# Last rounded layer of a 12-stage kernel: two of VectorE's steps move to GpSimd, one chunk ahead

## The reference, cut to what matters

```python
def _mx_quantize(t, eps=1e-30):                    # blocks of 32
    scales = maximum(max(abs(blocks), axis=-1) / 7.5, eps)
    q = nearest_on_grid(blocks / scales[..., None], GRID)   # 6-bit floats
    return q, scales
xq, xs = _mx_quantize(x2)
wq, ws = _mx_quantize(w2)
out = (xq * xs) @ (wq * ws).T + bias
...
x = x + 0.5 * _L3_ffn_ref(_layernorm(x), L3_ffn_weight, L3_ffn_bias)   # last line
```

## Time and profile before

| | |
|---|---|
| median of 3 runs | 2941.31 us |
| runs | 2941.31, 2930.59, 2941.32 us |
| the profiled execution's own time | 2940.02 us |
| its span in the profile | 2938.6 us |
| mean granted TensorE clock | 0.918 |

### The profile page before, as it was taken

How to read it: one execution, slowest core, us unless ns; L and a number is a source line. 1 busy time by engine, 2 the same in 40 slices (tenths; PEclk the granted TensorE clock), 3 DMA queues, 4 the chain that set the end, 5 groups by cost and what they waited for, 6 DMA issues and landing times.

```text
span 2938.6 us, 67913 instructions
## 1 busy us (share of the span) xinstructions
PE 2501.2 (85%) x25429; PEld 1983.4 (67%) x25429; DVE 2091.1 (71%) x7719; ACT 1766.2 (60%) x3449; POOL 1215.2 (41%) x1663
## 2 busy tenths in 40 slices
PE   7799998778699769459689999999999998895885
PEld 4467775455477547336479999999998896563664
DVE  6667765982377844664478888888988888446876
ACT  5444444533356334236369999999999995563553
POOL 4200002570274557575554442433244433556413
PEclk9789998978899879679889999999999998997997
DMA  9910000014310024225300000000010100441001
GB/s 237 277 44 3 3 3 1 6 46 128 110 34 14 31 76 137 80 88 160 109 19 16 19 21 14 21 14 14 14 35 23 36 23 12 131 147 31 25 6 30
DMA packets 126504, 164.60 MB, mean 56 GB/s; under 512 B 15457, under 2 KB 94946, under 8 KB 126178
## 3 DMA queue, kind: packets, MB, share of 16 engines
q1 hardware_dynamic: 98242, 86.58, 10.5%
q0 software_dynamic: 27936, 73.66, 8.3%
HBM read 85.18 MB, written 75.01 MB: 55 GB/s over the span
## 4 chain that ended last, share of the span: by engine, by line
PE 39%; DVE 13%; POOL 3%; issue 3%; ACT 1%; DMA 1%; DVEq 0%; POOLq 0%; ACTq 0%
PE banks L3643 7%; PE banks L3628 6%; PE banks L3573 3%; PE banks L3590 2%; PE banks L3609 2%; PE banks L3582 2%; PE banks L3566 2%; PE banks L3315 1%; PE banks L3317 1%; PE banks L3304 1%; PE banks L3305 1%; PE banks L3306 1%; PE banks L3608 1%; POOL bins L3269 1%; PE banks L3599 1%
## 5 line engine op out<-in xcount | busy, mean ns | idle before, releaser
L3643 PE MATMUL banks<-layer,shared_floats 128*128 128x128 f32 x2048 | 292.0, 275 | 0.0
L3643 PEld LDWEIGHTS banks<-layer,shared_floats 128*128 128x128 f32 x2048 | 258.8, 192 | 0.0
L3628 PE MATMUL banks<-shared_floats,layer 128*128 128x256 f32 x1024 | 243.9, 381 | 0.0
L4047 ACT ACTIVATE shared_floats<-banks,layer 128x256 f32<-128x256 f32 x512 | 210.1, 471 | 51.8 <-PE banks L3628 51.8
L3744 POOL TENSOR_SCALAR shared_floats<-shared_floats 128x2 f32<-128x2 f32 x256 | 58.2, 227 | 425.2 <-DVE shared_floats L3735 416.9
L3628 PEld LDWEIGHTS banks<-shared_floats,layer 128*128 128x128 f32 x1024 | 185.9, 192 | 20.2
L3746 POOL TENSOR_TENSOR shared_floats<-shared_floats,neg_half 128x2 f32<-128x2 f32 x256 | 184.1, 719 | 21.3
L3756 DVE TENSOR_SCALAR shared_floats<-banks,shared_floats 128x128 f32<-128x128 f32 x512 | 185.6, 404 | 6.9 <-POOL shared_floats L3746 6.9
L2213 DVE TENSOR_REDUCE shared_floats<-banks 128x2 f32<-128x512 f32 (+3 forms) x256 | 110.7, 485 | 93.1 <-PE banks L2077 91.7
L2318 ACT ACTIVATE shared_floats<-banks 128x480 f32<-128x480 f32 (+1 forms) x192 | 83.6, 488 | 143.9 <-PE banks L2084 143.9
L256 PE MATMUL banks<-ident,xn 128*128 128x128 f32 x320 | 61.1, 322 | 126.1 <-issue 76.3
(11 more groups left out here) (447 smaller groups left out, 7966.5 us busy)
## 6 DMA issues: line engine op xcount, KB each, us to landing
bins<-zero SPq DMA_DIRECT2D x1, 18176.0 KB, 69.7
layer<-in_dram_layers SPq DMA_DIRECT2D x16, 902.0 KB, 4.6
bins<-layer SPq DMA_DIRECT2D x16, 650.0 KB, 12.5
shared_floats<-bins SPq DMA_DIRECT2D x32, 325.0 KB, 3.9
expert_weights<-in_dram_experts SPq DMA_DIRECT2D x32, 312.0 KB, 3.1
outs<-shared_floats SPq DMA_DIRECT2D x16, 320.0 KB, 3.3
results<-zero SPq DMA_DIRECT2D x1, 4096.0 KB, 16.1
bins<-xn,f_bin_row POOLq DMA_INDIRECT x256, 2.3
```

What stands on the lines that cost most here:

```text
L3628: m = T.matmul(k.bank[5 + half][:, part], w["w1"][:, tile(n)], h1[:, :], start=True, stop=True)
L3643: m = T.matmul(to, hidden[:, n * S + t * P:n * S + (t + 1) * P], w["w2"][:, tile(n)], start=False, stop=(n == NF - 1), skip_group_check=True)
L4047: m = A.activation(hidden[:, n * S:(n + 1) * S], k.bank[5 + half][:, part], ACT.Gelu, bias=w["c1"][:, n:n + 1])
```

## The change

In the last stage alone, VectorE's rounding is split in three. `largest(i)` makes the scales and inverses, `widen(i)` the exponent bits, the magic number and its addition, and VectorE issues `largest(i + 1)` ahead of `widen(i)`. GpSimd makes the product with the inverse (`scale_blocks`, one chunk ahead) and the subtraction of the magic number (`subtract_magic`), before its multiplication by the scale. A second buffer each for the inverse and the magic number comes from arrays of the stage before, and ScalarE gets a wait for the product before it writes over a normalised buffer. `mix3` keeps `ffn3_quantise` as it was.

```diff
--- before.py
+++ after.py
@@ -828,6 +828,27 @@
     v.count(V.tensor_tensor(blocks(dst), blocks(src), spread(inverse), ALU.mult))
 
 
+def largest_of(k, src, scale, inverse, width):
+
+    V, v, nb = k.nc.vector, k.v, width // BLOCK
+    blocks = lambda ap: ap.rearrange("p (b k) -> p b k", k=BLOCK)
+    v.count(V.tensor_reduce(scale, blocks(src), AX.X, ALU.max, apply_absolute_value=True))
+    V.wait_ge(v.sem, v.n)
+    v.count(V.tensor_scalar(scale, scale, 1.0 / FP6_MAX, 1e-30, ALU.mult, ALU.max))
+    V.wait_ge(v.sem, v.n)
+    return V.reciprocal(inverse, scale)
+
+
+def add_magic(k, dst, magic):
+
+    V, v = k.nc.vector, k.v
+    v.count(V.tensor_scalar(magic.bitcast(U32), dst.bitcast(U32), 0x7F800000, None, ALU.bitwise_and))
+    V.wait_ge(v.sem, v.n)
+    v.count(V.tensor_scalar(magic, magic, 1.0, 1.5 * 2.0 ** 20, ALU.max, ALU.mult))
+    V.wait_ge(v.sem, v.n)
+    return V.tensor_tensor(dst, dst, magic, ALU.add)
+
+
 def to_six_bits(k, dst, magic):
 
 
@@ -878,6 +899,16 @@
     to_six_bits(k, xq[:, :], magic[:, :]).then_inc(k.sem("f3_rounded"), 1)
 
 
+def ffn3_inverse(k, n):
+
+    return (k.sb("f3_inverse", [P, CH // BLOCK]), k.sb("b3_tops", [P, 4 * BLOCKS]))[n % 2][:, 0:CH // BLOCK]
+
+
+def ffn3_magic(k, n):
+
+    return k.sb(("f3_magic", "b3_swapped")[n % 2], [P, CH])[:, :]
+
+
 def ffn3_multiply(k, engine, n):
 
     xq, scale = k.sb(f"f3_xq{n % 2}", [P, CH]), k.sb(f"f3_scale{n % 2}", [P, CH // BLOCK])
@@ -939,8 +970,24 @@
         V.scalar_tensor_tensor(out=k.chunk(i), in0=k.bank[4 + (s.c0 + i) % 2][:, :], scalar=0.5, in1=k.chunk(i),
                                op0=ALU.mult, op1=ALU.add).then_inc(k.sem("x_done"), 1)
 
+    def largest(i):
+        n = s.c0 + i
+        xn, inverse = k.sb(f"f3_xn{n % 2}", [P, CH]), ffn3_inverse(k, n)
+        V.wait_ge(k.sem("ln_xn"), s.ln(i) + 1)
+        if i >= 2:
+            V.wait_ge(k.sem("f3_scaled"), n - 1)
+        largest_of(k, xn[:, :], k.sb(f"f3_scale{n % 2}", [P, CH // BLOCK])[:, :], inverse, CH).then_inc(k.sem("l1_inverse"), 1)
+
+    def widen(i):
+        n = s.c0 + i
+        V.wait_ge(k.sem("l1_wide"), NC + i + 1)
+        add_magic(k, k.sb(f"f3_xq{n % 2}", [P, CH])[:, :], ffn3_magic(k, n)).then_inc(k.sem("f3_rounded"), 1)
+
+    largest(0)
     for i in range(NC):
-        ffn3_quantise(k, s, i)
+        if i + 1 < NC:
+            largest(i + 1)
+        widen(i)
         if i + 2 < NC:
             ln_stats(k, s, i + 2)
         if i:
@@ -953,6 +1000,8 @@
     k.nc.scalar.wait_ge(k.sem("x_done"), s.x0)
     ffn3_apply(k, s, 0)
     for i in range(NC):
+        if i + 1 >= 2 and i + 1 < NC:
+            k.nc.scalar.wait_ge(k.sem("l1_wide"), NC + i)
         if i + 1 < NC:
             ffn3_apply(k, s, i + 1)
         ffn3_copy(k, s.c0 + i, k.bank[2 + (s.c0 + i) % 2][:, :])
@@ -960,8 +1009,29 @@
 
 def ffn3_gpsimd(k, s):
 
+    G = k.nc.gpsimd
+
+    def scale_blocks(i):
+        n = s.c0 + i
+        xn, xq = k.sb(f"f3_xn{n % 2}", [P, CH]), k.sb(f"f3_xq{n % 2}", [P, CH])
+        G.wait_ge(k.sem("l1_inverse"), NC + i + 1)
+        G.wait_ge(k.sem("f3_turned"), n - 1)
+        G.tensor_tensor(tiles(xq[:, :], BLOCK), tiles(xn[:, :], BLOCK),
+                        ffn3_inverse(k, n).unsqueeze(2).broadcast_to([P, CH // BLOCK, BLOCK]), ALU.mult).then_inc(k.sem("l1_wide"), 1)
+
+    def subtract_magic(i):
+        n = s.c0 + i
+        xq = k.sb(f"f3_xq{n % 2}", [P, CH])
+        G.wait_ge(k.sem("f3_rounded"), n + 1)
+        k.g.count(G.tensor_tensor(xq[:, :], xq[:, :], ffn3_magic(k, n), ALU.subtract))
+        G.wait_ge(k.g.sem, k.g.n)
+
+    scale_blocks(0)
     for i in range(NC):
-        ffn3_multiply(k, k.nc.gpsimd, s.c0 + i)
+        if i + 1 < NC:
+            scale_blocks(i + 1)
+        subtract_magic(i)
+        ffn3_multiply(k, G, s.c0 + i)
         if i + 2 < NC:
             ln_shift(k, s, i + 2)
```

## The result

The changed kernel takes 2963.75 us, median of 5 runs (2956.59 to 2970.60); the kernel before, 2941.32 us in 5 runs beside it. The ratio is 1.0085, 95% interval 1.0067 to 1.0104: slower by 0.85%, as forecast (2965.9 us). The two medians lie 22.4 us apart, against 24.6 forecast. The profiled execution took 2967.28 us, its span 2965.8.

The account below looks back on a forecast made before the run. VectorE bounds the last stage at 5.96 us per chunk; the change closes a cross-engine ring of 9.09 plus 0.73 stall, 9.82 us, six times. With first and last turns it costs 24.6: 2941.3 becomes 2965.9 us, range 2952 to 2973.

Parts of the forecast that it names:

- to GpSimd, subtraction, to L916: Last stage: hand-over 0.09, GpSimd's subtraction 1.25, then 0.08 to its multiplication by the scale; 1.42 us.
- L916 to L191: Last stage, GpSimd: from the start of the multiplication by the scale to the start of the shift; 1.20 us.
- L191 to the end of L197: Last stage, GpSimd: the shift from first to last step, with VectorE idle beside it; 1.95 us.
- hand-over, norm, hand-over: Last stage: 0.09 to ScalarE, its four norms 1.65, 0.08 to VectorE; 1.82 us.
- The ring: Last stage: rounding chunk i queues behind a norm that follows from rounding chunk i - 1; 9.09 us, 9.82 with stall.
- The last turn: Last stage's final turn has no norm to wait for; chunk 7's multiplication ends 6.01 us after chunk 6's addition.
- The sum: Whole kernel: the change costs 24.6 us, so the median goes from 2941.3 to 2965.9 us, slower by 0.84%.
- The subtraction: GpSimd's subtraction of the magic number in the last stage, taken as 1.25 us between bounds 1.05 and 1.46.
- The stall: VectorE's rounding, starting second, waits for GpSimd's product to end; 0.73 us per turn, bounds 0 and 1.05.
- The rival in which GpSimd becomes the bound: Last stage: ring does not bind, GpSimd's own work sets 6.2 us a turn, 2945 us in all; chance 0.08.
- ScalarE's copy: Last stage: ScalarE's copy of chunk i lies beside GpSimd's shift and costs the ring nothing.
- The signs named for the profile: Last stage: VectorE's turn about 9.8 us, idle 4 to 5 us until the norm, subtraction near 1.25, L197 at 0.24.

Follow-up runs that it names:

- e3: Kernel before, nothing moved to GpSimd: VectorE makes scale, inverse and product of chunk i + 1 ahead of rounding chunk i; 2957.13 us, ratio 1.0058.
- e4: Changed kernel with GpSimd's product cut to the first 32 of 512 elements; 2955.36 us in one run.
- e7: Changed kernel with statistics and shift one chunk earlier, and ScalarE normalising chunk i + 2 ahead of its copy of chunk i; 2940.76 us, ratio 1.0004.
- e1: Changed kernel with statistics and shift made one chunk earlier; 2960.17 us, ratio 1.0066.
- e10: Changed kernel with only ScalarE's order changed, norm of chunk i + 2 ahead of the copy of chunk i; 2963.82 us in one run.
- e2: Changed kernel with VectorE rounding chunk i ahead of the block maximum of chunk i + 1, GpSimd's order kept; 2962.0 us in one run.
- e5: Kernel before in its old order, with only the subtraction of the magic number on GpSimd; 2929.21 us in one run.

## Why the prediction was right

The predicted median was 2965.9 us, the measured 2963.75. That the medians agree to 2 us is in part luck, since the start of the stage moves by more than that from profile to profile; what bears the prediction out are the steps inside the stage. By its own steps, in the changed kernel's turn from one addition (ends 2903.40) to the next (2913.09):

| step | predicted | measured |
|---|---|---|
| to GpSimd, subtraction, to L916 | 1.42 | 1.42 |
| L916 to L191 | 1.20 | 1.14 |
| L191 to the end of L197 | 1.95 | 1.96 |
| hand-over, norm, hand-over | 1.82 | 1.80 |
| block maximum, scale, inverse | 1.17 | 1.19 |
| exponent bits to the addition, with the stall | 2.26 | 2.18 |
| turn | 9.82 | 9.69 |

- **The ring**: right, and e3 shows it with nothing moved. The number of times it closes, six, is right too: chunk 0's addition ends 4.92 us after the stage's start (forecast 5.02), chunk 6's at 2951.81, so six turns take 58.1 us (58.9).
- **The last turn**: 6.01 us from chunk 6's addition to the end of chunk 7's multiplication, as forecast, with L845 at 1.11 and L847 at 1.15 us, both behind a GpSimd instruction. Behind it 7.98 us are left against 8.12 before.
- **The sum**: 24.6 forecast, 23.5 measured. The 1.1 us are 0.10 (first addition) + 0.83 (six turns) + 0.14 (what is left behind the last multiplication) from these lines.
- **The subtraction**: taken as 1.25 between bounds of 1.05 and 1.46; measured 1.26 to 1.27. The middle of two bounds was a choice, so that it fits to 0.02 is luck.
- **The stall**: forecast 0.73, and e4 takes 0.73 off the turn. The rows had only small instructions; at 128x512 on both sides the later one still waits to the other's end. The lock for a whole instruction that the Trainium skill describes in "SBUF — State Buffer" (Who interferes with whom) holds here: L847, 0.43 us long, took 1.15 beside L1019, which took 1.09 instead of 1.05.
- **The rival in which GpSimd becomes the bound**: its 6.2 us a turn is what e7 has, 6.20. But its condition was too weak. An earlier shift was named as enough; e1 shows that it leaves 9.27 us. And the total agrees better than its terms do: in e7 the product takes 1.00 up to the subtraction's start (counted 1.15), the multiplication up to L191 1.13 (1.20), the shift up to the next product 2.73 (2.50 with the 0.10 between).
- **ScalarE's copy**: it "lies beside the shift and costs nothing". In the changed kernel that is so (e10), by 0.3 us. It is the next bound, and the prediction didn't name it.

The signs named for the profile came out: a turn of 9.7 us (about 9.8 was named), L847 at 1.15, the subtraction at 1.26, VectorE idle 4.55 us ahead of the block maximum, ended by the norm; L197 at 0.24.

## What to carry to other kernels

A step issued one iteration ahead in an in-order queue makes everything behind it wait for that step's inputs. Before costing the moved work, follow the input back: if its producer stands at the end of the last iteration on another engine, the loop's turn becomes the whole chain, whatever each engine's busy time is. Look for the second ring as well, since opening one alone may give next to nothing (0.4 us a turn in e1, 0.03 in e10, and 0.65 in e2, which took the look-ahead out of one of two queues); and move look-ahead through all the queues (statistics, shift, norm) or through none.

## What the runs showed of the hardware that I had not expected

TensorE's clock may reach a loop that TensorE doesn't bound. The granted clock in the last stage was 0.76 before and is 0.63 after. TensorE in a turn after the change:

```profile
2906.02 1.08 PE L873 MATMUL banks<-ident,shared_floats 128*128 128x128 f32 x4 [4.56 <-POOL shared_floats L916]
...
2909.65 0.64 PE L884 MATMUL banks<-weightT,shared_floats 128*128 128x128 f32 x2
```

It stands idle for 4.56 us and then takes 0.64 us for a pair of 128x128 matmuls; from 2906.00 to 2911.20 the granted clock is 0.50 (1.2 GHz). Here that costs the ring nothing, as e10 shows: with the copy out of the norm's way the turn is the same. In e5 the two durations alternate together with VectorE's turns, and the expectation of e5, which counts TensorE nowhere, missed. That the clock makes the difference there is an estimate from e5's own rows. They alternate in the kernel before as well, and VectorE's turn stays 5.96 us:

```profile
2903.83 0.39 PE L863 MATMUL banks<-weightT,shared_floats 128*128 128x128 f32 x2
...
2911.57 0.63 PE L863 MATMUL banks<-weightT,shared_floats 128*128 128x128 f32 x2
```

The other point was foreseen from small instructions and now stands at this size: a blocked instruction has part of its time behind it when the block ends. The product ends 0.90 us after L845 (2911.18 to 2912.08), 0.15 less than the 1.05 it takes alone, and L847 ends 0.29 us after the product (2912.37), 0.14 less than its 0.43. Together they are 1.19 us, as the forecast counted, where the two in a row would be 1.05 + 0.43 = 1.48.
